# D's diagonals behind the table's, and the two decode stages of a fused Mamba and LUT-FFN layer in another order

## The reference

```
x = u                                               # [4, 1024, 512]
proj = layernorm(x) @ W_in.T                        # z 512, x 512, B 64, C 64, dt 8
xBC  = silu(causal depthwise conv over 4 tokens + conv_b)
dt   = softplus(dt + dt_bias);  A = -exp(A_log)
S_t  = S_(t-1) * exp(dt A) + dt * B x;  y = S_t C + D * x      # 8 heads of 64, state 64
x = x + layernorm((y * silu(z)) @ W_out.T)
w = lut[idx]                                        # 16 levels; gate, up, down of 512 x 1376
x = x + layernorm((silu(x_n @ gate.T) * (x_n @ up.T)) @ down.T), x_n = layernorm(x)
```

## Time and profile before

| | us |
|---|---|
| median of 3 runs | 1380.91 (1380.16 to 1382.7) |
| the profiled execution | 1378.51 |
| its span, first to last instruction | 1376.7 |
| PE busy | 1308.4 (95%) |
| DVE busy | 948.5 (69%) |
| ACT busy | 554.1 (40%) |
| POOL busy | 492.7 (36%) |

### The profile page before, as it was taken

One profiled execution on the slowest core, in us unless ns is written; L12 is line 12 of the kernel. 1 busy time (PEld: TensorE's weight loads), 2 busy tenths in 40 slices (PEclk: granted clock), 3 DMA queues, 4 the chain that ended last, 5 costly groups with the idle time before them and its releaser, 6 DMA issues. The chain is left out here.

```text
span 1376.7 us, 18802 instructions
## 1 busy us (share of the span) xinstructions
PE 1308.4 (95%) x6720; PEld 639.6 (46%) x6720; DVE 948.5 (69%) x1889; ACT 554.1 (40%) x1042; POOL 492.7 (36%) x701
## 2 busy tenths in 40 slices
PE   2889998998999999999999999999999999999997
PEld 1345455544444444444444444444444445444443
DVE  6888977897688657875687558766886565544342
ACT  4577676775434323332334243424342223132120
POOL 2222233324434544444434533354345334401102
PEclk9999999999999999999999999999999999999999
DMA  5054235323321342122302430232113112311201
GB/s 171 1 134 116 81 95 142 98 73 74 77 54 31 96 96 54 32 69 70 85 23 62 107 85 24 59 102 68 49 31 100 49 36 61 93 31 35 73 0 54
DMA packets 132812, 96.16 MB, mean 70 GB/s; under 512 B 102000, under 2 KB 102000, under 8 KB 132720
## 3 DMA queue, kind: packets, MB, share of 16 engines
q1 hardware_dynamic: 124752, 78.74, 22.2%
q10 hardware_dynamic: 7968, 16.23, 4.3%
HBM read 54.05 MB, written 16.78 MB: 51 GB/s over the span
## 5 line engine op out<-in xcount | busy, mean ns | idle before, releaser
L1430 PE MATMUL bank<-fxt,ffn_hi 128*128 128x512 f16 (+1 forms) x1408 | 419.0, 379 | 9.6 <-DVE gact L1770 7.9
L1430 PE MATMUL bank<-fxt,ffn_lo 128*128 128x512 f16 (+1 forms) x704 | 266.8, 379 | 0.0
L1430 PEld LDWEIGHTS bank<-fxt,ffn_hi 128*128 128x128 f16 (+1 forms) x1408 | 139.6, 100 | 179.5 <-DVE gact L1770 10.9
L651 POOL TENSOR_TENSOR state<-state,ex 64x512 f32<-64x512 f32 x32 | 37.5, 1171 | 268.9 <-PE bank L1387 267.8
L1444 PE MATMUL bank<-ffn_hi,h_hi 128*128 128x512 f16 (+1 forms) x352 | 133.5, 379 | 0.0
L1444 PE MATMUL bank<-ffn_hi,h_lo 128*128 128x512 f16 (+1 forms) x352 | 133.4, 379 | 0.0
L1444 PE MATMUL bank<-ffn_lo,h_hi 128*128 128x512 f16 (+1 forms) x352 | 133.3, 379 | 0.0
L1324 PE MATMUL bank<-mask,diag 128*128 128x416 f16 x640 | 122.2, 347 | 9.9 <-ACT ffn_lo L926 9.2
L1643 DVE SCALAR_TENSOR_TENSOR xs<-cin,conv_w_sb,xs 128x512 f32<-128x512 f32 x114 | 105.6, 927 | 19.2 <-ACT xs L869 16.1
L978 ACT ACTIVATE gact<-bank,c_gate_half 128x512 f32<-128x512 f32 (+1 forms) x88 | 59.9, 681 | 146.2 <-PE bank L1430 144.4
L1770 DVE SCALAR_TENSOR_TENSOR gact<-gact,bank 128x512 f32<-128x512 f32 (+1 forms) x88 | 60.2, 684 | 84.6 <-ACT gact L978 83.7
(11 more groups left out here) (195 smaller groups left out, 2218.2 us busy)
## 6 DMA issues: line engine op xcount, KB each, us to landing
codes_sb<-codes ACTq DMA_DIRECT2D x76, 208.0 KB, 3.4
ures<-u SPq DMA_DIRECT2D x32, 256.0 KB, 3.0
x_scratch<-x SPq DMA_DIRECT2D x32, 256.0 KB, 2.4
ut<-x_scratch SPq DMA_DIRECT2D x16, 512.0 KB, 4.4
xres<-x_scratch SPq DMA_DIRECT2D x32, 256.0 KB, 3.0
out<-dn SPq DMA_DIRECT2D x32, 256.0 KB, 2.0
ut<-u SPq DMA_DIRECT2D x15, 512.0 KB, 4.3
ffn_hi<-w_in_t SPq DMA_DIRECT2D x4, 580.0 KB, 8.6
```

The lines of the kernel that those rows point to most:

```text
L1430: last = nc.tensor.matmul(bank, wt[:, c0:c0 + w], fxt[:, :, half, k, :], start=(k == 0 and n == 0), stop=(k == KC - 1 and n == 2))
```

## The change

Nothing is computed otherwise, and no instruction of work is added or taken away. `decode_stage` is gone from all five engines; its two calls are written out step by step in a new order, and the setup in front of them is reordered too. POOL makes D's diagonals behind the table's, with one wait more between their two halves. The partition maximum of W_in stands ahead of the last `ln_split`, a's scaling ahead of c_in's half, and `segments(0, 0)` ahead of `pair_rstd("u", 1, 0)`. On SP the first pair of tile 1 is loaded ahead of the codes. In the stages, `y_sum` and `y_gated` stand ahead of the masks of the chunk, `decoded` comes between the parts of `small` and `decays`, `dt_exponential`, `out_projected` and some `decays` come later, and scans stand behind other numbers of decode units: chunk 1 of stage 0 has units 5 to 7, chunk 2 units 8 to 13; in stage 1 scan (1, 1) comes behind unit 3, scan (1, 2) behind unit 9, scan (1, 3) behind unit 13. Conversions of codes stand in direct pairs at (2, 3), (10, 11), (12, 13), (17, 18), (20, 21), (26, 27), (30, 31), (33, 34) and (38, 39). On SP, `residual(0, 3)` stands ahead of `transpose_y(0, 3)`. Stages from 2 on are the same text. The diff, cut to the start, most of stage 0 and the first steps of stage 1; in the order SP, POOL, ACT, PE, DVE:

```diff
+                load_pair("u", 1, 0)
                 load_codes(0)
                 load_codes(1)
-                load_pair("u", 1, 0)
...
+                transpose_y(0, 0)
+                load_pair("u", 1, 1)
+                transpose_pair("u", 1, 0)
+                transpose_pair("u", 1, 1)
+                load_pair("u", 2, 0)
+                residual(0, 0)
...
+                transpose_y(0, 2)
+                residual(0, 2)
+                store_x1(0, 1)
+                residual(0, 3)
+
+                transpose_y(0, 3)
+                store_x1(0, 2)
+                store_x1(0, 3)
+                transpose_pair("u", 2, 0)
+                load_pair("u", 2, 1)
...
+                    pool.wait_ge(s_diag, 1)
+                    for b in range(2):
+                        rows = slice(b * NST, (b + 1) * NST)
+                        nc.gpsimd.tensor_tensor(
+                            d_diag[rows], ident[rows, :].unsqueeze(1).broadcast_to((NST, KC, P)),
+                            d_sb[rows, :].rearrange("p (k b) -> p k b", b=2)[:, :, b:b + 1].broadcast_to((NST, KC, P)),
+                            ALU.mult).then_inc(s_ddiag, 1)
+                        pool.wait_ge(s_ddiag, b + 1)
...
                 pair_rstd("u", 0, 0)
                 pair_rstd("u", 0, 1)
-                pool.wait_ge(s_small, 64)
-                for b in range(2):
...
-                pool.wait_ge(s_ddiag, 2)
                 pool.wait_ge(s_lowest, 1)
                 nc.gpsimd.partition_all_reduce(big[:, 0:1], lowest[:, 0:1], P, RMAX).then_inc(s_all, 1)
                 pool.wait_ge(s_wbig, 1)
                 nc.gpsimd.partition_all_reduce(big[:, 1:2], lowest[:, 1:2], P, RMAX).then_inc(s_wall, 1)
...
+                table_diagonals()
+                d_diagonals()
+                segments(0, 0)
                 pair_rstd("u", 1, 0)
-                segments(0, 0)
                 weigh_x(0, 0)
-                for t in range(LAG):
-                    decode_stage(t)
+                decay_state(0, 0)
+                segments(0, 1)
+                weigh_x(0, 1)
+                pair_rstd("u", 1, 1)
+
...
+                decay_state(0, 3)
+                out_rstd(0, 2)
+                segments(1, 0)
+                pair_rstd("u", 2, 0)
+                weigh_x(1, 0)
+                add_residual(0, 2)
+
+                decay_state(1, 0)
+                segments(1, 1)
+                out_rstd(0, 3)
+                add_residual(0, 3)
+                pair_rstd("u", 2, 1)
+                weigh_x(1, 1)
...
                 act.dma_start(conv_w_sb[:], conv_w.rearrange("(f p) k -> p f k", p=P)).then_inc(s_small, 16)
                 normalise_slice("u", 0, 0, 0)
                 normalise_slice("u", 0, 0, 1)
+                normalise_slice("u", 0, 1, 0)
+                normalise_slice("u", 0, 1, 1)
                 slice_transposed(0)
-                normalise_slice("u", 0, 1, 0)
                 slice_transposed(1)
-                normalise_slice("u", 0, 1, 1)
+                a_exponential()
                 slice_transposed(2)
                 slice_transposed(3)
...
+                high_half(0)
+                high_half(1)
+                high_half(2)
+                dt_input(0)
                 conv_input(0, 4)
-                dt_input(0)
                 conv_input(0, 0)
+                conv_tanh(0, 4)
                 dt_exponential(0)
-                conv_tanh(0, 4)
+                conv_tanh(0, 0)
+                codes_to_half(0)
                 high_half(3)
-                conv_tanh(0, 0)
+                z_tanh(0, 0)
                 conv_input(0, 1)
-                act.wait_ge(s_pair, 1)
-                z_tanh(0, 0)
                 conv_input(0, 2)
+                z_tanh(0, 1)
                 conv_input(0, 3)
-                codes_to_half(0)
                 conv_tanh(0, 1)
-                z_tanh(0, 1)
                 conv_tanh(0, 2)
+                decays(0, 0)
                 small_sums(0, 0)
-                decays(0, 0)
+                z_tanh(0, 2)
                 conv_tanh(0, 3)
-                z_tanh(0, 2)
                 small_x(0, 0)
...
+                small(0, 1)
+                decoded(0, 0)
+                codes_to_half(4)
+                decoded(0, 1)
+                decoded(0, 2)
+                codes_to_half(5)
+                decoded(0, 3)
+                decays(0, 1)
+                codes_to_half(6)
+                decoded(0, 4)
+                normalise_slice("u", 1, 1, 0)
+                normalise_slice("u", 1, 1, 1)
+                codes_to_half(7)
+                out_projected(0, 0)
+                dt_input(1)
+                codes_to_half(8)
+                decoded(0, 5)
+                normalise(0, 0)
+                conv_input(1, 4)
+                small(0, 2)
+                decays(0, 2)
+                conv_tanh(1, 4)
+                codes_to_half(9)
+                conv_input(1, 0)
+                decoded(0, 6)
+                codes_to_half(10)
+                codes_to_half(11)
+                decoded(0, 7)
+                dt_exponential(1)
+                out_projected(0, 1)
+                conv_tanh(1, 0)
+                codes_to_half(12)
+                codes_to_half(13)
+                decoded(0, 8)
+                decoded(0, 9)
+                conv_input(1, 1)
+                decoded(0, 10)
+                decoded(0, 11)
+                codes_to_half(14)
+                small(0, 3)
+                decays(0, 3)
+                codes_to_half(15)
...
+                scan(0, 0)
+                prepare(0, 1)
+                decode(0, 0)
+                segment_sums(0, 1)
+                decode(0, 1)
+                decode(0, 2)
+                decode(0, 3)
+                decode(0, 4)
+
+                scan(0, 1)
+                project_out(0, 0)
+                decode(0, 5)
+                segment_sums(0, 2)
+                project_dt(1)
+                project_conv(1, 4)
+                prepare(0, 2)
+                project_conv(1, 0)
+                decode(0, 6)
+                project_out(0, 1)
+                decode(0, 7)
+
+                scan(0, 2)
+                decode(0, 8)
+                project_conv(1, 1)
+                decode(0, 9)
+                decode(0, 10)
+                decode(0, 11)
+                segment_sums(0, 3)
+                prepare(0, 3)
+                project_conv(1, 2)
+                project_conv(1, 3)
+                project_out(0, 2)
+                decode(0, 12)
+                decode(0, 13)
+
+                scan(0, 3)
+                decode(0, 14)
+                decode(0, 15)
+                project_z(1, 0)
+                prepare(1, 0)
+                segment_sums(1, 0)
+                decode(0, 16)
+                decode(0, 17)
+                project_z(1, 1)
+                decode(0, 18)
+                project_out(0, 3)
+
+                scan(1, 0)
+                project_z(1, 2)
+                project_z(1, 3)
+                decode(0, 19)
+                prepare(1, 1)
+                decode(1, 0)
+                decode(1, 1)
+                segment_sums(1, 1)
+                decode(1, 2)
+                project_out(1, 0)
...
-                    ln_split("u", 0, k // 2, k % 2)
+                    if k + 1 < KC:
+                        ln_split("u", 0, k // 2, k % 2)
                 dve.wait_ge(s_big, KC)
                 nc.vector.tensor_reduce(lowest[:, 0:1], win_max[:], AX_X, ALU.max).then_inc(s_lowest, 1)
+                ln_split("u", 0, 1, 1)
...
+                scale_a()
+                half_scale()
+                low_half(0)
+                low_half(1)
+                low_half(2)
+                table_rows()
+                wout_partitions()
                 conv(0, 4)
                 dt_input(0)
-                dve.wait_ge(s_wall, 1)
-                scales(1)
-                nc.vector.tensor_scalar(c_out[:], c_in[:], expo[:, 1:2], 0.25 / (WS * WS), ALU.mult,
-                                        ALU.mult).then_inc(s_wscale, 1)
+                clear_state(0)
+                wout_scale()
                 conv(0, 0)
                 conv_silu(0, 4)
                 conv_silu(0, 0)
                 time_steps(0)
                 conv(0, 1)
-                ln_stats("u", 1, 0)
                 z_gate(0, 0)
                 conv(0, 2)
+                ln_stats("u", 1, 0)
                 conv_silu(0, 1)
                 conv(0, 3)
                 conv_silu(0, 2)
-                clear_state(0)
+                conv_silu(0, 3)
                 z_gate(0, 1)
-                conv_silu(0, 3)
+                z_gate(0, 2)
                 weigh(0, 0)
                 decayed(0, 0)
-                z_gate(0, 2)
+                z_gate(0, 3)
+
+                y_sum(0, 0)
+                y_gated(0, 0)
                 masks(0)
-                z_gate(0, 3)
-                for t in range(LAG):
```

(35 more changed lines are left out.)

## The result

| | before | after |
|---|---|---|
| median of 4 runs, us | 1381.59 (1380.16 to 1382.70) | 1366.80 (1365.32 to 1367.52) |
| profiled execution, us | 1378.51 | 1367.52 |
| its span, us | 1376.7 | 1365.8 |

The ratio is 0.9888 with a 95% interval from 0.9873 to 0.9903: 14.8 us faster, against a forecast of 14.4 us.

What follows compares the result with a forecast made beforehand. The prediction took TensorE as the bound, with about 30 us above its floor in the two decode stages. Start 2.4 plus stages 12 made 14.4 us, so 1380.9 became 1366.5 us, range 1357 to 1379.

Steps and rivals of the forecast that it cites:

- The maximum of the weights: POOL's start: first all-reduce 3.4 us earlier (ends 0 and 8.5), first projection 3.2 us earlier, at 27.5.
- rival 2: At the start, the all-reduce's load overlaps its wait: first projection 8.5 us earlier, total 1361.4 us; chance 0.15.
- From the first projection to the first scan: Setup: fourth silu at 66 sets the first scan, 2.4 us earlier at 66.6; POOL's diagonals cost DVE 2.55 us.
- So the slow clock is paid once here too: 0.: At the first scan: PE idles about as long as before, so slow clock moves from segment sums to scan, net 0.
- The stages: Two decode stages: new order removes PE waits and slow clock; 12 us counted, ends 0 and 18.
- The bound of 30.8 us: Two decode stages: 19.8 us of PE idle time plus at most 11 us of slow clock above the floor.
- The walk: New stage queues followed operation by operation without semaphore delays: 10.8 us new waits, 3.2 us slow clock, net 16.8 us.
- the 4.8 us held back: Two decode stages: taken off the net 16.8 us for semaphore delays, POOL and DVE blocking and DVE at 85%.
- three signs of being wrong: PE's stage waits staying near 19.8 us, PE waiting for y's fourth transpose, or first projection at 30.
- Rival 3: Decode stages: ACT's nine conversion pairs wait for codes and pass 37 us to PE, total 1384.7 us; chance 0.08.
- Rival 1: Only the start pays; waits removed in the stages return behind masks or y_sum, total 1378.5 us; chance 0.06.
- rival 4: Partial compensation: half of the gain in the stages, 6 us, total 1372.5 us; chance 0.16.

Runs made afterwards that it cites:

- e3: The new kernel with 24 matmuls, their result thrown away, filling PE's 5.2 us wait in front of the first x transposes; 1363.5 us, ratio 0.9866.
- e5: The new kernel's decode stages behind the setup of the kernel before; 1370.0 us, ratio 0.9911.
- e9: The kernel before with PE's queue alone changed: project_out (0, 0) behind scan (0, 1) instead of in front of it; 1383.4 us, ratio 1.0008.
- e10: The kernel before with ACT's queue alone changed, in stage 1: copies of unit 2 ahead of normalise (0, 3) and u (2)'s slices; 1386.7 us, ratio 1.0027.
- e11: The kernel before with PE's queue alone changed: decode unit 11 ahead of prepare and segment sums of chunk 3, both stages; 1381.0 us, ratio 0.9987.
- e1: The kernel before with one edit: D's diagonals made behind the table's on POOL; 1378.2 us, ratio 0.9972.

## Why the prediction was right, and where not

**The total** (14.4 us forecast, 14.8 measured) and the two parts of the sum (2.4 for the start, 12 for the stages) agree with what each part does alone, 3.5 and 12.2 us. The chain by which the start's 2.4 us were reached was wrong in two steps that offset each other: 5.7 us too little at the first scan (8.1 against 2.4), and 5.8 us left out behind it. That the sum for the start came out near the measured one is luck.

**The maximum of the weights.** The step failed. Of the ends 0, 3.4 and 8.5 us I took 3.4, because the pause seemed to follow whatever went before it. It was the far end: the all-reduce came 8.35 us earlier (17.57 against 25.92) and the first projection 7.9. I had it as rival 2 at 0.15. Its gain at the first scan, 7.5 us, was nearly right (8.1); its total of 1361.4 was 5.4 us too low, about what the clock cost. The argument that "the maximum was long ready before, so no row can tell" was right about the row, and an open question should have got more than 0.15. In the new kernel POOL is free from 11.74; the pause of 5.65 us ends at 17.4 and the maximum is there at 16.89, so an earlier maximum would have gained little more.

**From the first projection to the first scan.** 39.1 us forecast, 38.2 measured. The fourth silu was what came next, as foreseen. POOL's blocking was mis-sized: D's diagonals cost DVE 1.5 us (two products of 1.41 and 1.43 us instead of 0.69), not 2.55, and the table's 1.6 us on three taps, as much as before on another operation. Each half of D (1.3 and 1.4 us) had run some 0.5 us before DVE's product began, and cost it 0.7 us, not its full length.

**"So the slow clock is paid once here too: 0."** The step failed. PE had the same idle time as before (5.23 against 5.17 us), but not the same work behind it. The low clock lasted from 60 to 77 us instead of some 6 us, and cost 5.8 us (e3). This ate all that the start had won beyond the forecast.

**The stages.** The bound of 30.8 us was read rightly, and that 12 of it could be had was right in size (e5: 12.2). The walk behind it was right only in part. `segment_sums(0, 2)` waits 1.3 us against 1.2, and xt's transpose costs 1.8 against 1.0. The waits for ACT's copies sum to 4.5 us against 6.6, but not where the walk had them: units 9 and 11 of stage 0 wait 0.4 us together, units 13 and 15 wait 1.4 and 0.6, and unit 5 of stage 1 waits 1.6. The 1.5 us in front of scan (0, 1) did not come. And the 2.0 us in front of `project_out(0, 0)`, which the text gives to y's transpose, were a wait for W_out's low half: y's transpose was issued at 82.5 and takes some 3 us, while DVE ended the low half at 97.9 and PE started at 98.0. It missed y's transpose (0, 3): by the walk it was issued at 182.8 and had 1 us to spare, and it was issued at 187.15 and took 6.8 us to PE instead of 3.1. A step with 1 us to spare after 120 us of a walk without delays should have been priced. It missed 2.4 us behind z's gates, and 13.0 us that ACT's conversions now wait for DVE's masks (1.1 us before). In sum 16.9 us of waits stand against 10.8, and the 4.8 us held back for what the walk leaves out were nearly the missing 6.1; that they were is luck, too.

**The signs.** Of those that the forecast gave, these came: ACT's waits for codes (17.7 us against about 20), the start of stage 1 (197.95 against no later than 198), and an idle PE ahead of the x transposes, though at 59.9 and not 66. These did not: the all-reduce at 22.6 (17.57), the first projection at 27.5 (22.77), the scan of stage 2 at 326 to 333 (335.91), a clock above 0.96 in both stages (0.92 and 1.00), and a DVE operation of 2 us or more at 41 to 46 (the longest of that time takes 1.4). Of the three signs of being wrong one came: y's fourth transpose is PE's longest wait, 3.5 us. A second was near: PE's waits in the stages fell only from 19.8 to 16.9 us. A forecast that gets the time and misses these has the right total for partly wrong reasons.

**That single waits have single prices** is the part that the experiments take back. The text gave each wait of the earlier trace rows to one reordering. Made alone, three of these moves changed nothing (e9), cost 3.6 us (e10) and gained 2 us that are not clear of nothing (e11). As far as these three show, the 12 us belong to the set.

**Rivals.** Rival 3's mechanism is there and didn't bind: ACT's waits for codes are

```profile
ACT codes_h L944 <- DMA codes_sb<-codes: 17.7, 6, 4.6
```

(forecast about 20), and PE's waits for its copies still fell from 9.2 to 4.5 us. Rival 1 (only the start pays) is what the two traces look like; e5 rules it out, and rival 4 (6 us in the stages) with it: its interval, 0.9895 to 0.9926, is 10 to 15 us.

## What to carry to other kernels

A difference of two traces tells where time went in these two schedules, not which edit earned it: taking each half of a change alone told that 12 of 15 us came from stages whose length had hardly changed. Before pricing an idle gap by its length, look at what runs behind it: here 5.2 us of idle in front of x transposes and a scan cost 5.8 us more by the clock, and 24 matmuls thrown away bought that back in the chunk; how much of it reaches the total is less sure (3.3 us by the medians). In queues that wait for each other, one list moved alone may only pick another step to be late, as it did in three tries here. A sum that comes out right says little of its terms: two of these were each off by nearly 6 us.

## What was not expected of the hardware

POOL's pause in front of the first all-reduce (5.65 us) can run while POOL waits for the all-reduce's input: with an empty queue the all-reduce started 0.4 us (e1) and 0.7 us (the new kernel) behind the input. After the second all-reduce a pause of 6.8 to 7.2 us stands in front of the table's diagonals in before, e1 and the new kernel alike. After 5.2 us of idle time, TensorE's granted clock stayed at 0.50 from 60 to 77 us in the new kernel, with no wait over 0.8 us in between; the work was x transposes and a scan in 32-bit matmuls, then small sums and a decode unit. Before, behind the same 5.2 us but with segment sums (32-bit, too) and a projection of 512 columns next, it was low for some 6 us. What in the work makes the difference was not taken apart: e3 shows only that with the idle time filled, the clock over the same scan is 1.00.
